# One weight piece subtracted and written ahead of four norms, and one up product ahead of the second turn of h

## What is computed

```python
def _L0_ffn_ref(x, gate_w, up_w, down_w, gate_scale, up_scale, down_scale):
    B, S, H, I = (1, 64, 256, 768)
    def _quantized_matmul(x, w, scale):
        wq = w.astype(jnp.float8_e4m3fn).astype(x.dtype)
        y = jnp.einsum('bsi,io->bso', x, wq)
        return y * scale
    gate = jax.nn.silu(_quantized_matmul(x, gate_w, gate_scale))
    up = _quantized_matmul(x, up_w, up_scale)
    fuse = gate * up
    return _quantized_matmul(fuse, down_w, down_scale)
...
x = x + 0.5 * _L0_ffn_ref(_layernorm(x, axis=-1), ...)
x = x + _L0_attn_ref(_layernorm(x, axis=-1), ...)
x = x + 0.5 * _L0_ffn_ref(_layernorm(x, axis=-1), ...)
```

## Time and profile before

| what | value |
|---|---|
| median of 3 runs | 154.87 us (154.87 to 154.97) |
| profiled execution, its own time | 155.3 us |
| its span | 153.5 us |
| PE busy | 147.2 us (96% of the span) |
| DVE busy | 121.4 us (79%) |
| ACT busy | 85.2 us (56%) |
| POOL busy | 68.5 us (45%) |
| granted clock of PE | 1.00 over the whole span |

### The profile page before, as it was taken

One profiled execution on the slowest core, in us unless ns is written; L12 is line 12 of the kernel. 1 busy time (PEld: TensorE's weight loads), 2 busy tenths in 40 slices (PEclk: granted clock), 3 DMA queues, 4 the chain that ended last, 5 costly groups with the idle time before them and its releaser, 6 DMA issues.

```text
span 153.5 us, 3712 instructions
## 1 busy us (share of the span) xinstructions
PE 147.2 (96%) x1327; PEld 117.4 (76%) x1327; DVE 121.4 (79%) x271; ACT 85.2 (56%) x203; POOL 68.5 (45%) x76
## 2 busy tenths in 40 slices
PE   5999899999999999998999999999999999999992
PEld 2366588788989696967686969698877788888991
DVE  0797999999799485859688888899755999566784
ACT  2385998677232453547475656657676648453310
POOL 3447244775891700283845748573978220000000
PEclk9999999999999999999999999999999999999999
DMA  4999502903000000000000000000000000002114
GB/s 112 339 354 306 214 0 31 361 27 121 15 0 0 4 0 4 0 4 0 4 2 0 6 0 6 0 4 0 4 2 0 0 4 0 0 0 68 34 36 139
DMA packets 7009, 8.47 MB, mean 55 GB/s; under 512 B 448, under 2 KB 5712, under 8 KB 6992
## 3 DMA queue, kind: packets, MB, share of 16 engines
q1 hardware_dynamic: 6816, 8.16, 16.0%
q10 hardware_dynamic: 176, 0.07, 0.4%
HBM read 7.19 MB, written 1.05 MB: 54 GB/s over the span
## 4 chain that ended last, share of the span: by engine, by line
PE 74%; POOL 10%; DVE 6%; issue 4%; ACT 3%; DMA 2%; POOLq 0%; ACTq 0%; DVEq 0%
PE bank L1167 23%; PE bank L1195 14%; PE bank L1223 9%; POOL grstd L340 6%; PE bank L1280 5%; PE bank L1236 5%; PE bank L1250 4%; PE bank L1364 3%; PE bank L1309 3%; DMA xt<-in_L_attn_x 2%; POOL rstd L318 2%; PE bank L1262 2%; DVE stats L705 2%; PE bank L1296 1%; PE bank L1341 1%
## 5 line engine op out<-in xcount | busy, mean ns | idle before, releaser
L1167 PE MATMUL bank<-hh,up_r 128*128 128x512 f32 x92 | 25.5, 401 | 0.1
L1167 PE MATMUL bank<-hh,gate_r 128*128 128x512 f32 x92 | 25.6, 401 | 0.0
L1195 PE MATMUL bank<-down_r,fhi 128*128 128x256 f32 x96 | 24.3, 291 | 0.0
L340 POOL TENSOR_TENSOR grstd<-gve,neg_half 128x16 f32<-128x16 f32 x8 | 23.3, 2908 | 0.7
L1195 PE MATMUL bank<-down_r,flo 128*128 128x256 f32 x96 | 23.4, 281 | 0.0
L455 ACT ACTIVATE gact<-bank,vec 128x512 f32<-128x512 f32 x24 | 16.3, 684 | 9.0 <-PE bank L1167 8.1
L463 ACT ACTIVATE fhi<-fuse 128x512 fp32r<-128x512 f32 x24 | 14.6, 624 | 10.8 <-DVE fuse L752 10.8
L1167 PEld LDWEIGHTS bank<-hh,up_r 128*128 128x128 f32 x92 | 16.8, 188 | 4.3 <-issue 0.6
L1167 PEld LDWEIGHTS bank<-hh,gate_r 128*128 128x128 f32 x92 | 16.9, 188 | 4.0 <-ACT gate_r L404 0.4
L1195 PEld LDWEIGHTS bank<-down_r,fhi 128*128 128x128 f32 x96 | 18.1, 188 | 0.7 <-issue 0.2
L1195 PEld LDWEIGHTS bank<-down_r,flo 128*128 128x128 f32 x96 | 18.1, 188 | 0.6 <-issue 0.2
(11 more groups left out here) (90 smaller groups left out, 285.6 us busy)
## 6 DMA issues: line engine op xcount, KB each, us to landing
raw<-in_rotation SPq DMA_DIRECT2D x1, 1536.0 KB, 7.5
out<-xt SPq DMA_DIRECT2D x8, 128.0 KB, 1.8
raw<-in_L_ffn_down_w SPq DMA_DIRECT2D x2, 384.0 KB, 7.4
wqkv<-in_L_attn_w_qkv SPq DMA_DIRECT2D x1, 768.0 KB, 9.3
xt<-in_L_attn_x SPq DMA_DIRECT2D x2, 256.0 KB, 3.7
xt<-in_L_attn_x SPq DMA_DIRECT2D x1, 512.0 KB, 5.4
raw<-in_rotation SPq DMA_DIRECT2D x1, 512.0 KB, 3.5
raw<-in_L_ffn_gate_w SPq DMA_DIRECT2D x1, 384.0 KB, 6.2
```

The source lines that it names most:

```text
L340: pool.tensor_tensor(grstd[:, c % 2], gve[:, :], neg_half[:, :], ALU.pow).then_inc(grstd_done, 1)
L1167: mm = pe.matmul(dst[:, :], wr[m][:, k * I + i * P:k * I + (i + 1) * P], half[:, k, g % NG, :], start=(k == 0 and half is hhi), stop=(k == ...
L1195: mm = pe.matmul(downs[d][:, 0:C], half[:, g % NG, i, t * P:(t + 1) * P], wr["down"][:, i * C:(i + 1) * C], start=(i == 0 and half is fhi) ...
```

## The change

Three calls are moved, each within the list of its own engine; nothing is added or removed, and POOL's and SP's lists are the same.

```diff
@@ -557,11 +557,11 @@
             to_weights(2)
             silu(0)
+            to_weights(3)
             norm_act(4)
             norm_act(5)
             norm_act(6)
             norm_act(7)
-            to_weights(3)
             split_h(1, 0)
             split_h(1, 1)
@@ -893,8 +893,8 @@
             grid_step(4)
             grid_add(3)
+            subtract(3)
             shift_rows(2)
-            subtract(3)
             fuse_up(0)
@@ -1377,8 +1377,8 @@
             gate_up(1, ("gate",))
             gate_up(2, ("gate",))
+            gate_up(1, ("up",))
             turn_h(1)
-            gate_up(1, ("up",))
             gate_up(2, ("up",))
```

## The result

The changed kernel takes 155.13 us (median of 22 runs, 154.98 to 155.29), the one before 154.90 in the same session (22 runs, 154.80 to 155.03). The ratio is 1.0014, 95% interval 1.0008 to 1.0020: 0.22 us slower, between 0.12 and 0.31. The forecast was +0.15.

A forecast was written before the change was run, and what follows sets the result against it. The prediction took DVE, busy 15.47 of 15.60 us up to 34.6, to set PE's time. Subtraction 0, late norms +0.15 and up part 0 gave +0.15 us: 154.87 to 155.0, likeliest case 154.9 to 155.2, full range 154.5 to 155.6.

The forecast's parts named there:

- Subtraction: 0: On DVE, the subtraction of piece 3 fits into the wait for POOL's power and costs the shift 0.
- Block at POOL, the slower rival: Subtraction and POOL's power hold each other up, first norm +0.71 or +0.86, time 155.6 to 155.7 us; chance 0.19.
- Write ahead of the norms: 0.15 late: On ACT, writing piece 3 first delays norms, last transposes and high parts by 0.15 us; 0.26 without overlap.
- Up part ahead of the transposes: PE gains 0.3: On PE, moving product 1's up part forward starts the third matmul of product 3's gate part 0.3 us earlier.
- The hold ahead of product 8: PE's gap ahead of the up part of product 8 was to grow from 0.09 to about 0.4 us.
- The gain is given back at DVE's fuses: PE's gain is lost waiting for fuse_up(6) and fuse_up(8), which come 0.15 us later; product 10's up part at 34.93.
- Sum +0.15: At the kernel's end, the parts together cost +0.15 us, median 154.87 to 155.0.
- DVE's gap: Ahead of the rests of h, DVE is done about 0.6 us earlier but waits for ACT, gaining its chain nothing.

The follow-up runs named there:

- e1: Kernel before with only DVE's subtraction of piece 3 moved ahead of the shift; ratio 0.9996 to the kernel before.
- e9: Kernel before with subtraction of piece 3 ahead of the shift, grid_clip(5) ahead of the rests of h, grid_step(6) ahead of fuse_up(4); ratio 1.0005.
- e2: Kernel before with the subtraction and the write of piece 3 moved, PE's list as before; ratio 1.0008 to the kernel before.
- e4: Changed kernel with silu(1) moved ahead of the high parts on ACT; ratio 1.0008 to the kernel before.
- e3: Changed kernel with grid_clip(5) moved ahead of the rests of h on DVE; ratio 0.9986 to the kernel before.
- e8: Kernel before with only PE's up part of product 1 moved ahead of the transposes; ratio 1.0214 to the kernel before.

## Why the prediction was right, point by point

- **Subtraction: 0.** Right. It ran 0.72 behind the addition's start (forecast 14.05 - 13.33 = 0.72) for 0.69, with 0.20 us to spare ahead of the shift. e1: no change at any point.
- **Block at POOL, the slower rival.** It didn't occur in the changed kernel: power 1.37, subtraction 0.69. The Trainium skill's rule on the first issuer (SBUF — State Buffer, Who interferes with whom) holds for POOL's subtraction in e9, but not for a power under way in the changed kernel, where the measurement decides: the subtraction starts 0.51 behind the power and keeps its 0.69, as the product beside a power did. That a power's reads are over long before it ends would explain it; it is inferred from the durations, not seen.
- **Write ahead of the norms: 0.15 late.** Right, 0.18 at the norms, 0.16 at the rests of h; e2 shows that it is the whole cost.
- **Up part ahead of the transposes: PE gains 0.3.** Wrong. PE gained 0.04 at product 3 (6.39 against 6.43). And these 0.04 don't come from the moved up part, since e2 has 6.38 without it. I had made the gate part of product 3 wait for the high parts and its third matmul for the rests, but left out its bank: `gate_up(3)` waits for `silu(1)`, which stands behind the high parts on ACT, 0.91 us of waiting on PE. e4 shows the wait and what it is worth: 0.67 at the first matmul, 0.10 at the next part. The hold ahead of product 8 grew to 0.23 and not to the forecast 0.4, as the gain that was to be lost there hadn't been made.
- **The gain is given back at DVE's fuses.** Right, and shown from three sides: e4 frees PE and the end stays (+0.01), e3 frees DVE and the end comes 0.41 earlier, e8 delays the rests of h by 2.89 and the end by 2.86. The sum had the gain consumed there, so the error of the step above didn't reach it.
- **Sum +0.15.** Measured +0.22 (0.12 to 0.31) by the ratio, +0.13 in the trace. The two agree within the interval; no run explains the 0.09 between them.
- **DVE's gap.** The forecast said that the 0.6 us which DVE has in hand ahead of the rests of h gives nothing to its chain. True for this order of calls (the gap grew from 0.21 to 0.92 and the rests came no earlier), and the wrong place to stop: moving one clip into it turns 1.0014 into 0.9986.

## What to carry to other kernels

When a chain of waits names one engine at a stall, look for the engine that is full behind it: here PE stood waiting for a weight piece, but the time of everything after was set by DVE, which had 0.13 us of room in 15.6. Work moved into a wait opens a gap where it stood, and in these runs it paid only once something was put there: the change left 0.53 us idle on ACT and 0.92 on DVE. The three moves cost 0.13 in the trace, and one clip in DVE's gap gave 0.41. And list every condition of the next instruction, its output buffer too, before counting what an engine gains.

## What the runs showed of the hardware

- A power on POOL under way (1.37 us for four columns) doesn't hold up a DVE subtraction with two SBUF inputs (0.69), while a POOL subtraction under way turns a DVE step of 0.55, which reads one, into one of 1.47 (e9).
- 2.3 us without work on PE, in the midst of a kernel that otherwise keeps 1.00, were followed by granted clocks of 0.73 and 0.53 over 4.7 us, and a stall that I had put at 1.8 us was one of 2.9 (e8). By the estimate there, about 0.8 of the 1.1 is the clock.
